# Cross stage: the parts of q and k in one DRAM array, stored by one transfer; the stacks loaded head by head

## The chip, the cores and the metric

The kernel runs on one core of one Trainium2 chip. The metric is the device time of one execution in microseconds (us).

## The reference

A decoder layer with normalisation after each block, on 32 sequences (batches) of 256 tokens and 256 features, and a context of 120 rows for each sequence:

```python
x = layernorm(x + self_attention(x))          # 16 heads of 16, rotary
x = layernorm(x + cross_attention(x, ctx))    # 16 heads, differential
x = layernorm(x + feed_forward(x))            # 64 experts, top 6, and a shared one
```

The change lies in the cross attention. There each head has two softmaxes:

```python
q1, q2 = (q[..., :8], q[..., 8:])             # q, k: heads of 16
k1, k2 = (k[..., :8], k[..., 8:])
a1 = softmax(einsum('bhtd,bhsd->bhts', q1, k1) * SCALING)
a2 = softmax(einsum('bhtd,bhsd->bhts', q2, k2) * SCALING)
out = einsum('bhts,bhsd->bhtd', a1 - lam * a2, v)
```

## The kernel before

The kernel has three stages, one after the other: self attention, cross attention, feed forward. The two attention stages are pipelines over the batches. In step t the cross stage loads x and ctx of batch t (X), projects q and k of batch t-1 (A), loads the stacks of batch t-2 and starts its maxima of the scores (B), finishes those of batch t-3 (M), computes scores, exponentials and values of batch t-4 (S), and later phases follow (O, R, Q). Each step of each engine is written out by hand, in eight sub-steps, and each engine works through its own list in order, waiting on semaphores.

To keep float32 accuracy in bf16 matmuls, q and k are split into three bf16 parts whose sum is the float32 value (`cparts`, made by `copy_parts0`, `copy_parts1` on ScalarE and two subtractions on GpSimd). A score is the sum of six products of parts. The six are laid below one another in a stack, so that one matmul with a contraction over 48 rows (6 pairs x 8 features) does them: `q_stack` and `k_stack`, 48 rows for each half `e` of the head (e = 0 at partition 0, e = 1 at partition 64), and along the free dimension all 16 heads, 256 queries or 120 keys each.

`cparts` has (feature, head) in the partitions, feature-major, and the stacks want the feature in the partition and the head in the free dimension. SyncE's queue makes this turn through DRAM: the phase A of a step stores the parts of batch t-1 (L586, L588), and the phase B of the next step loads them back as stack rows (L556), 7 loads for each e: of q 8, 8, 16 and 16 rows, of k 24, 16 and 8 rows (`C_STACK_LOADS`). Before the change each of q and k has its own DRAM array with e outermost, `[3, E, NP, P, T]` and `[3, E, NP, P, KEYS]` (3 slots, 2 halves, 3 parts, 128 rows of (feature, head), then queries or keys). There a stack row, one feature of all 16 heads, is a single run of 16 x 256 x 2 = 8192 bytes (q) or 16 x 120 x 2 = 3840 bytes (k).

SyncE issues in this order in a step: x and ctx for X, the residual for S, then, after the stores of the step before have landed (`c_pw`), the 14 stack loads for B; y and its transpose x2T for R; the three row loads of `cnmaxT` for M (L569, after ScalarE's copy); gates and counts for Q (L574, L576); and at last the four stores of parts for A, after `c_lo`. TensorE waits for all 14 loads (`c_st`) before `cross_max_scores(B, 0)` (L829), in the sixth of the eight sub-steps, and behind it come the other maxima, the transpose of the maxima L1021 that M needs, and the values. ScalarE's `copy_parts0` waits for the stores of the step before, since it overwrites `cparts`.

The self stage makes the same turn with arrays of its own, which the change does not touch.

Of the kernel before, what the change touches and what calls it, by code (L numbers as in the profile page):

```python
# [8 lines left out]
BF16 = mybir.dt.bfloat16  # L9
# [4 lines left out]
P = 128  # L14
DM = 256
T = 256
TC = T // P
FC = DM // P
NH = 16
# [3 lines left out]
NP = 3  # L23
# [11 lines left out]
def past(b, n):  # L35

    return True if not isinstance(b, int) else b >= n
# [7 lines left out]
def held(eng, count):  # L45


    if isinstance(count, int):
        return count
    register = eng.alloc_register()  # L50
    eng.reg_mov(register, count)
    return register
# [50 lines left out]
def attention(nc, n_batches, x_in, xT_in, W, ctxT_in, CW, consts, y_out, res_out, z_out, yT_out, counts_out, moe, ident, ahead, count):  # L103
# [24 lines left out]
    for is_q in (True, False):  # L128
        part_of = [pair[0 if is_q else 1] for pair in PAIRS]
        at = 0  # L130
# [17 lines left out]
    KEYS = ctxT_in.shape[1]  # L148
    E = 2
# [5 lines left out]
    HALF = P // E  # L155
    KPAD = P - KEYS
    QW, KW = E * T, E * KEYS
# [6 lines left out]
    for is_q in (True, False):  # L164
        part_of = [pair[0 if is_q else 1] for pair in PAIRS]
        at = 0
# [9 lines left out]
    cres_rows = res_out.rearrange("(b c p) d -> b p c d", p=P, c=TC)  # L176
    ctxT_rows = ctxT_in.rearrange("(b f p) n -> b p f n", f=FC, p=P)
    cy_rows = z_out.rearrange("(b c p) d -> b p c d", p=P, c=TC)
    cq_dram = nc.dram_tensor("cross_q_parts", [3, E, NP, P, T], BF16, kind="Internal").ap()
    ck_dram = nc.dram_tensor("cross_k_parts", [3, E, NP, P, KEYS], BF16, kind="Internal").ap()  # L180

    with ExitStack() as ctx:
        def sb(label, shape, dt=F32):
            return ctx.enter_context(nc.sbuf_tensor(f"att_{label}", shape, dt))
# [3 lines left out]
        def sem(label):  # L188
            sems.append(nc.alloc_semaphore(f"att_{label}"))
            return sems[-1]  # L190
# [28 lines left out]
        q_stack = sb("q_stack", [P, 3, NH * T], BF16)  # L219
        k_stack = sb("k_stack", [P, 3, NH * T], BF16)  # L220
# [41 lines left out]
        cparts = parts[:, :, :, :, :].rearrange("p z t c n -> p (z t c n)")[:, 0:NP * (QW + KW)]\  # L262
# [93 lines left out]
        c_pw = [sem(f"cross_parts_written{p}") for p in range(3)]  # L356
        c_st = [sem(f"cross_stacks_loaded{p}") for p in range(3)]
# [53 lines left out]
        def _(sp):  # L411
# [100 lines left out]
            def cross_step(at_lag):  # L512
                X, A, B, M, S, R, Q = (at_lag(lag) for lag in (0, 1, 2, 3, 4, 6, 7))
# [26 lines left out]
                        sp.wait_ge(c_sum, S.n - 2)  # L540
                    sp.dma_start(x_res[:, S.slot, :, :], cres_rows[S.n]).then_inc(c_res_in[S.slot], 16)
                if B.on:
                    n_pw = held(sp, 64 * (B.turn + 1))
                    sp.wait_ge(c_wts, 16)
                    sp.wait_ge(c_pw[B.slot], n_pw)

                    if not past(B.n, 3):
                        sp.wait_ge(c_ones, B.n + 1)
                    if past(B.n, 3):
                        sp.wait_ge(c_sc, NGR * (B.n - 2))  # L550
                    for e in range(E):
                        q_src = cq_dram[B.slot][e].rearrange("t (d h) n -> (t d) (h n)", h=NH)
                        k_src = ck_dram[B.slot][e].rearrange("t (d h) n -> (t d) (h n)", h=NH)
                        for is_q, row, src_row, m in C_STACK_LOADS:
                            stack, src, n = (q_stack, q_src, T) if is_q else (k_stack, k_src, KEYS)
                            sp.dma_start(stack[e * HALF + row:e * HALF + row + m, B.slot, 0:NH * n],  # L556
                                         src[src_row:src_row + m, :]).then_inc(c_st[B.slot], 16)
                if R.on:
                    sp.wait_ge(c_y, R.n + 1)
                    sp.dma_start(cy_rows[R.n][:, :, 0:DM], y_sb[:, R.slot, :, :]).then_inc(c_stored[R.slot], 16)  # L560
# [17 lines left out]
                if A.on:  # L578
                    n_lo = held(sp, A.n + 1)
                    sp.wait_ge(c_wts, 16)  # L580
                    sp.wait_ge(c_lo, n_lo)

                    if past(A.n, 3):
                        sp.wait_ge(c_st[A.slot], 16 * C_N_ST * A.turn)
                    for e in range(E):
                        sp.dma_start(cq_dram[A.slot][e].rearrange("t p n -> p t n"),  # L586
                                     cparts[:, :, e * T:(e + 1) * T]).then_inc(c_pw[A.slot], 16)
                        sp.dma_start(ck_dram[A.slot][e].rearrange("t p n -> p t n"),  # L588
                                     cparts[:, :, QW + e * KEYS:QW + (e + 1) * KEYS]).then_inc(c_pw[A.slot], 16)

            run_both(sp, step, cross_step, n_batches, LAGS, C_LAGS)
            sp.wait_ge(c_ahead, 16 * (len(ahead) + P // n_batches))
            sp.wait_ge(s_zero, 16 * len(moe) * (n_batches + 1))
# [471 lines left out]
        def _(act):  # L1065
# [125 lines left out]
            def copy_parts0(A, last):  # L1191
                act.wait_ge(c_ke, 2 * (A.n + 1))
                act.wait_ge(c_qe, 2 * (A.n + 1))

                if past(A.n, 1):
                    act.wait_ge(c_pw[last.slot], 64 * (last.turn + 1))
                else:
                    for p in range(3):
                        act.wait_ge(s_pw[p], 32 * len(range(p, n_batches, 3)))
                act.activation(cparts[:, 0, :], cqk[:, :], ACT.Copy).then_inc(c_hi, 1)  # L1200
# [5 lines left out]
            def cross_step(at_lag):  # L1206
# [59 lines left out]
                if A.on and not shared(A):  # L1266
                    copy_parts0(A, at_lag(2))
# [38 lines left out]
                if A.on and shared(A):  # L1306
                    copy_k(A)
                    copy_parts0(A, at_lag(2))
# [920 lines left out]
```

## Time and profile before

| | |
|---|---|
| time, median of 3 runs | 1919.88 us (1917.16 to 1926.09) |
| the profiled execution: time | 1924.67 us |
| the profiled execution: span | 1922.6 us |
| mean granted TensorE clock | 0.946 |
| TensorE busy | 1690.0 us (88%) |
| VectorE busy | 1310.4 us (68%) |
| share of the 16 DMA engines that SyncE's queue takes | 62.0% |

PE is TensorE's matmuls, PEld its weight loads, DVE VectorE, ACT ScalarE, POOL GpSimd, SP SyncE; a q behind a name is the engine's queue of issued transfers. L829 is line 829 of the kernel. The cross stage runs from about 720 to 1520 us of the span; from 830 to 1410 us all its phases are active. "Busy" leaves out issuing and waiting; a DMA packet is one piece that one of the 16 engines moves, and the share of the DMA is the mean over the 16.

### The profile page before, as it was taken

Reading aid. Unit: us, or ns where it says so; the run is one execution under the profiler, and the core shown is the slowest. Engines: PE = TensorE matmul, PEld = TensorE weight load, DVE = VectorE, ACT = ScalarE, POOL = GpSimd, SP = SyncE. Lnnn points to the kernel's source line nnn. Section 1 sums busy time; section 2 is a strip of 40 time slices with the busy share of each in tenths; the row PEclk is TensorE's granted clock in tenths of the full one; section 3 lists DMA queues with packets and bytes.
Section 4 is the critical chain, followed back from the end, with each engine's and each line's share of the span. In section 5 each row is a group of like instructions: output and inputs, shape, how many; then the busy total and the mean of one; then the engine's idle time right before and its main releaser. Section 6 shows DMA issues by size and latency. Waiting matters only on the chain. (4 is left out here: it accounts for less than half of the span.)

```text
span 1922.6 us, 43658 instructions
## 1 busy us (share of the span) xinstructions
PE 1690.0 (88%) x14562; PEld 1183.5 (62%) x14562; DVE 1310.4 (68%) x2959; ACT 1083.8 (56%) x1701; POOL 858.5 (45%) x788
## 2 busy tenths in 40 slices
PE   3789999999999997889989989999898749999985
PEld 2566667666666665555556555555555438888774
DVE  3566776777666775668888887988888544444275
ACT  1466666666666665567777777777776501111244
POOL 4567776777666742211212111111211005887565
PEclk6899999999999999899999999999998759999998
DMA  5577767776777666566655566566664326887686
GB/s 121 132 190 184 193 168 196 188 188 170 195 189 188 169 172 144 123 119 132 139 132 128 127 129 125 136 133 141 135 125 87 90 59 177 197 195 196 178 292 218
DMA packets 312751, 302.79 MB, mean 157 GB/s; under 512 B 68842, under 2 KB 289836, under 8 KB 303304
## 3 DMA queue, kind: packets, MB, share of 16 engines
q1 hardware_dynamic: 302408, 288.66, 62.0%
q0 software_dynamic: 10240, 12.81, 3.9%
q8 instruction: 59, 0.97, 0.2%
q14 instruction: 44, 0.36, 0.1%
HBM read 188.36 MB, written 112.00 MB: 156 GB/s over the span
## 5 line engine op out<-in xcount | busy, mean ns | idle before, releaser
L1340 DVE TENSOR_REDUCE att_nmax<-self_p_mx 128x2 f32<-128x512 f32 x512 | 328.8, 686 | 203.3 <-PE self_p_mx L629 202.8
L1430 DVE TENSOR_REDUCE att_cross_nmax<-self_p_mx 128x8 f32<-128x960 f32 x256 | 294.4, 1150 | 86.5 <-PE self_p_mx L829 85.4
L1074 ACT ACTIVATE att_probs<-self_p_sc 128x1024 f32<-128x1024 f32 x256 | 261.3, 1021 | 98.5 <-PE self_p_sc L617 96.2
L1167 ACT ACTIVATE att_probs<-self_p_sc 120x1024 f32<-120x1024 f32 x256 | 261.9, 1023 | 65.4 <-PE self_p_sc L811 64.5
L629 PE MATMUL self_p_mx<-att_k_stack,att_q_stack 96*128 96x256 bf16 x1024 | 160.8, 277 | 54.5 <-DMA att_k_stack<-self_k_parts 49.2
L847 PE MATMUL self_p_pv<-att_probs,att_v_aug 120*32 120x256 f32 x2048 | 172.3, 410 | 0.0
L617 PE MATMUL self_p_sc<-att_q_stack,att_k_stack 99*128 99x256 bf16 x1024 | 158.5, 278 | 11.4 <-ACT att_probs L1074 10.0
L829 PE MATMUL self_p_mx<-att_k_stack,att_q_stack 48*128 48x120 bf16 x2048 | 101.2, 220 | 70.6 <-DMA att_k_stack<-cross_k_parts 37.9
L1683 POOL TENSOR_SCALAR att_cross_var_eps<-att_cross_mv 128x2 f32<-128x2 f32 x32 | 7.2, 226 | 332.3 <-DVE att_cross_mv L1536 289.7
L1697 POOL TENSOR_TENSOR att_qk_rest<-att_qk,att_parts 128x752 f32<-128x752 f32 x32 | 51.8, 1619 | 214.3 <-ACT att_parts L1200 214.3
L629 PEld LDWEIGHTS self_p_mx<-att_k_stack,att_q_stack 96*128 96x128 bf16 x1024 | 96.0, 98 | 82.9 <-DMA att_k_stack<-self_k_parts 35.3
L617 PEld LDWEIGHTS self_p_sc<-att_q_stack,att_k_stack 99*128 99x128 bf16 x1024 | 87.1, 98 | 91.1 <-ACT att_probs L1074 42.7
L644 PE MATMUL self_p_pv<-att_probs,att_v_aug 128*32 128x256 f32 x2048 | 141.9, 396 | 0.5 <-ACT att_probs L1074 0.5
L829 PEld LDWEIGHTS self_p_mx<-att_k_stack,att_q_stack 48*128 48x128 bf16 x2048 | 70.0, 97 | 107.5 <-DVE att_cross_nmax L1430 56.2
L1904 PE MATMUL ffn_p<-shared_w,ffn_hT 128*128 128x256 f32 x512 | 122.3, 393 | 12.4 <-ACT ffn_hT L1967 12.0
L1913 PE MATMUL ffn_ph<-ffn_xT,shared_w 128*128 128x256 f32 x512 | 118.9, 386 | 0.0
L1904 PEld LDWEIGHTS ffn_p<-shared_w,ffn_hT 128*128 128x128 f32 x512 | 97.9, 196 | 31.3 <-ACT ffn_hT L1967 17.5
L1637 POOL TENSOR_TENSOR att_rope_products<-att_qkb,att_cos_t 128x512 f32<-128x512 f32 x32 | 40.9, 1279 | 154.8 <-ACT att_qkb L1090 154.8
L2090 POOL DMA_INDIRECT expert_sums<-ffn_ye,ffn_slots x64 | 92.3, 1442 | 37.3 <-issue 14.7
L1177 ACT ACTIVATE att_o_raw<-self_p_pv 128x512 f32<-128x512 f32 x128 | 75.8, 592 | 56.3 <-PE self_p_pv L847 56.3
L1701 POOL TENSOR_TENSOR att_parts<-att_qk_rest,att_parts 128x752 bf16<-128x752 f32 x32 | 51.7, 1614 | 124.9 <-ACT att_parts L1204 124.9
L1967 ACT ACTIVATE ffn_hT<-ffn_ph 128x512 f32<-128x512 f32 x64 | 37.7, 594 | 121.5 <-PE ffn_ph L1913 87.8
(180 smaller groups left out, 3682.4 us busy)
## 6 DMA issues: line engine op xcount, KB each, us to landing
att_q_stack<-self_q_parts SPq DMA_DIRECT2D x64, 256.0 KB, 5.7
expert_sums<-att_zeros SPq DMA_DIRECT2D x64, 256.0 KB, 8.7
att_q_stack<-cross_q_parts SPq DMA_DIRECT2D x128, 128.0 KB
ffn_w<-in_ffn_w SPq DMA_DIRECT2D x64, 256.0 KB
ffn_m_sb<-expert_sums SPq DMA_DIRECT2D x32, 512.0 KB, 6.0
self_q_parts<-att_parts SPq DMA_DIRECT2D x32, 384.0 KB
self_k_parts<-att_parts SPq DMA_DIRECT2D x32, 384.0 KB
att_k_stack<-self_k_parts SPq DMA_DIRECT2D x32, 384.0 KB, 7.9
```

Of the source, the lines that this page charges most:

```text
L617: mm = pe.matmul(p_sc[:, w, kc * T:(kc + 1) * T], k_stack[0:RM, S.slot, k_at:k_at + P], q_stack[0:RM, S.slot, u * T:(u + 1) * T], start=Tr ...
L629: mm = pe.matmul(p_mx[:, m % 2, c * T:(c + 1) * T], q_stack[0:RK, M.slot, q_at:q_at + P], k_stack[0:RK, M.slot, m * T:(m + 1) * T], start= ...
L644: mm = pe.matmul(p_pv[j * SLOT:(j + 1) * SLOT, (p % 2) * T:(p % 2 + 1) * T], v_aug[:, S.slot, kc, u, :], probs[:, (u // 2) % 4, (2 * (u % ...
L829: mm = pe.matmul(p_mx[:, e, (2 * hh + c) * KEYS:(2 * hh + c + 1) * KEYS], q_stack[r:r + C_RK, M.slot, q_at:q_at + P], k_stack[r:r + C_RK, ...
L847: mm = pe.matmul(p_pv[j * SLOT:(j + 1) * SLOT, (g % 2) * T:(g % 2 + 1) * T], v_aug[0:KEYS, S.slot, e, 2 * g + hh, :], probs[0:KEYS, g % 4, ...
L1074: act.activation(probs[:, g % 4, :], p_sc[:, :, :].rearrange("p b n -> p (b n)"), ACT.Exp, scale=SCALE).then_inc(s_exp, 1)
L1167: act.activation(probs[0:KEYS, g % 4, :], p_sc[0:KEYS, :, :].rearrange("p b n -> p (b n)"), ACT.Exp, scale=C_SCALE).then_inc(c_exp, 1)
L1340: dve.tensor_reduce(nmax[:, M.slot, :, m], p_mx[:, m % 2, :].rearrange("p (c k) -> p c k", c=TC), AX_X, ALU.max, negate=True).then_inc(s_r ...
L1430: dve.tensor_reduce(cnmax[:, M.slot, :, :, 2 * m:2 * m + 2].rearrange("p c e h -> p e h c"), p_mx[:, :, 0:4 * KEYS].rearrange("p e (x k) - ...
L1904: mm = pe.matmul(p_y[:, tc * DM:(tc + 1) * DM], hT[:, b % 2, k, tc * P:(tc + 1) * P], sw2[:, k, :], start=(k == 0), stop=(k == SK - 1))
L1913: mm = pe.matmul(p_h[:, k // 2, (k % 2) * T:(k % 2 + 1) * T], sw1[:, f, k * P:(k + 1) * P], xT[:, t % 3, f, :], start=(f == 0), stop=(f == ...
L2090: pool.indirect_dma_start(out=moe[j][:, :], out_offset=bass.IndirectOffsetOnAxis(ap=slots[:, e:e + 1], axis=0), in_=ye[:, k % 3, j, :], in ...
```

## The change

The two DRAM arrays become one, `cross_parts`, `[3, NP, P, QW + KW]`: for each part and each (feature, head) one run of 2 x 256 + 2 x 120 = 752 elements (1504 bytes), as `cparts` has it. One transfer stores it, in place of four, and the counts of `c_pw` go from 64 to 16 for each batch. The 14 stack loads stay, with the same rows; each reads 16 runs (one for each head) of 512 or 240 bytes for a stack row, 1504 bytes apart.

```diff
--- before.py
+++ after.py
@@ -176,8 +176,7 @@
     cres_rows = res_out.rearrange("(b c p) d -> b p c d", p=P, c=TC)
     ctxT_rows = ctxT_in.rearrange("(b f p) n -> b p f n", f=FC, p=P)
     cy_rows = z_out.rearrange("(b c p) d -> b p c d", p=P, c=TC)
-    cq_dram = nc.dram_tensor("cross_q_parts", [3, E, NP, P, T], BF16, kind="Internal").ap()
-    ck_dram = nc.dram_tensor("cross_k_parts", [3, E, NP, P, KEYS], BF16, kind="Internal").ap()
+    c_dram = nc.dram_tensor("cross_parts", [3, NP, P, QW + KW], BF16, kind="Internal").ap()
 
     with ExitStack() as ctx:
         def sb(label, shape, dt=F32):
@@ -540,7 +539,7 @@
                         sp.wait_ge(c_sum, S.n - 2)
                     sp.dma_start(x_res[:, S.slot, :, :], cres_rows[S.n]).then_inc(c_res_in[S.slot], 16)
                 if B.on:
-                    n_pw = held(sp, 64 * (B.turn + 1))
+                    n_pw = held(sp, 16 * (B.turn + 1))
                     sp.wait_ge(c_wts, 16)
                     sp.wait_ge(c_pw[B.slot], n_pw)
 
@@ -548,13 +547,13 @@
                         sp.wait_ge(c_ones, B.n + 1)
                     if past(B.n, 3):
                         sp.wait_ge(c_sc, NGR * (B.n - 2))
+                    by_row = c_dram[B.slot].rearrange("t (d h) n -> (t d) h n", h=NH)
                     for e in range(E):
-                        q_src = cq_dram[B.slot][e].rearrange("t (d h) n -> (t d) (h n)", h=NH)
-                        k_src = ck_dram[B.slot][e].rearrange("t (d h) n -> (t d) (h n)", h=NH)
                         for is_q, row, src_row, m in C_STACK_LOADS:
-                            stack, src, n = (q_stack, q_src, T) if is_q else (k_stack, k_src, KEYS)
-                            sp.dma_start(stack[e * HALF + row:e * HALF + row + m, B.slot, 0:NH * n],
-                                         src[src_row:src_row + m, :]).then_inc(c_st[B.slot], 16)
+                            stack, at, n = (q_stack, e * T, T) if is_q else (k_stack, QW + e * KEYS, KEYS)
+                            dst = stack[e * HALF + row:e * HALF + row + m, B.slot, 0:NH * n]
+                            sp.dma_start(dst.rearrange("p (h n) -> p h n", h=NH),
+                                         by_row[src_row:src_row + m, :, at:at + n]).then_inc(c_st[B.slot], 16)
                 if R.on:
                     sp.wait_ge(c_y, R.n + 1)
                     sp.dma_start(cy_rows[R.n][:, :, 0:DM], y_sb[:, R.slot, :, :]).then_inc(c_stored[R.slot], 16)
@@ -582,11 +581,8 @@
 
                     if past(A.n, 3):
                         sp.wait_ge(c_st[A.slot], 16 * C_N_ST * A.turn)
-                    for e in range(E):
-                        sp.dma_start(cq_dram[A.slot][e].rearrange("t p n -> p t n"),
-                                     cparts[:, :, e * T:(e + 1) * T]).then_inc(c_pw[A.slot], 16)
-                        sp.dma_start(ck_dram[A.slot][e].rearrange("t p n -> p t n"),
-                                     cparts[:, :, QW + e * KEYS:QW + (e + 1) * KEYS]).then_inc(c_pw[A.slot], 16)
+                    sp.dma_start(c_dram[A.slot].rearrange("t p n -> p t n"), cparts[:, :, :])\
+                      .then_inc(c_pw[A.slot], 16)
 
             run_both(sp, step, cross_step, n_batches, LAGS, C_LAGS)
             sp.wait_ge(c_ahead, 16 * (len(ahead) + P // n_batches))
@@ -1193,7 +1189,7 @@
                 act.wait_ge(c_qe, 2 * (A.n + 1))
 
                 if past(A.n, 1):
-                    act.wait_ge(c_pw[last.slot], 64 * (last.turn + 1))
+                    act.wait_ge(c_pw[last.slot], 16 * (last.turn + 1))
                 else:
                     for p in range(3):
                         act.wait_ge(s_pw[p], 32 * len(range(p, n_batches, 3)))
```

## Rows read from the trace of the kernel before

**Rows 1.** The page: the span, and busy time of each engine (share of span, instructions)

```profile
span 1922.6 us, 43658 instructions
PE 1690.0 (88%) x14562; PEld 1183.5 (62%) x14562; DVE 1310.4 (68%) x2959; ACT 1083.8 (56%) x1701; POOL 858.5 (45%) x788
```

**Rows 2.** The waits, whole span: us in total, times, longest us

```profile
PE self_p_mx L829 <- DMA att_k_stack<-cross_k_parts: 37.9, 23, 6.3
...
PEld self_p_mx L829 <- DMA att_k_stack<-cross_k_parts: 16.5, 8, 6.6
```

**Rows 3.** The waits, 830 to 1410 us

```profile
PE self_p_mx L829 <- DMA att_k_stack<-cross_k_parts: 27.2, 19, 2.9
...
PEld self_p_mx L829 <- DMA att_k_stack<-cross_k_parts: 4.1, 3, 1.9
```

**Rows 4.** The waits of SyncE's queue, 830 to 1410 us

```profile
SPq L569 <- ACT att_cross_nmaxT L1314: 168.9, 25, 9.5
...
SPq L545 <- DMA cross_k_parts<-att_parts: 14.2, 14, 1.7
SPq L550 <- DMA cross_k_parts<-att_parts: 6.3, 5, 1.9
```

**Rows 5.** The windows: busy time of the engines, 830 to 1410 us

```profile
core 0: us, PE busy (x) PEld busy (x) DVE busy (x) ACT busy (x) POOL busy (x), PEclk, DMA share, GB/s
830.00:1410.00 580.00, 527.32 (x5750) 337.58 (x5750) 492.61 (x1146) 421.96 (x702) 114.92 (x150) 0.98 0.63 132
```

**Rows 6.** The timeline of SyncE's queue: start us, us

```profile
1033.41 1.70 SPq L569 DMA_DIRECT2D att_q_stack<-att_cross_nmaxT  x3
...
1036.77 0.40 SPq L586 DMA_DIRECT2D cross_q_parts<-att_parts  x1
...
1038.31 0.51 SPq L588 DMA_DIRECT2D cross_k_parts<-att_parts  x1
1039.16 0.38 SPq L532 DMA_DIRECT2D att_xT<-x  x1
...
1042.05 1.46 SPq L556 DMA_DIRECT2D att_q_stack<-cross_q_parts  x4
...
1046.21 1.13 SPq L556 DMA_DIRECT2D att_k_stack<-cross_k_parts  x3
```

**Rows 7.** The timeline of TensorE: start us, us; in brackets the idle time before

```profile
1053.80 0.39 PE L829 MATMUL self_p_mx<-att_k_stack,att_q_stack 48*128 48x120 bf16 x8 [0.70 <-DMA att_k_stack<-cross_k_parts]
...
1055.18 0.28 PE L1021 MATMUL self_p_k<-att_identb,att_cross_nmax_parts 128*96 128x128 bf16 x2
```

**Rows 8.** The DMA view, 288.5 to 290.5 us (the self stage stores its parts)

```profile
DMA packets 1037, 0.52 MB, mean 261 GB/s; under 512 B 16, under 2 KB 1037, under 8 KB 1037
...
q1 hardware_dynamic: 1037, 0.52, 89.2%
```

**Rows 9.** The DMA view, 302.7 to 303.7 us (rows of 1024 bytes)

```profile
DMA packets 388, 0.37 MB, mean 375 GB/s; under 512 B 22, under 2 KB 388, under 8 KB 388
...
q1 hardware_dynamic: 388, 0.37, 108.1%
```

**Rows 10.** The DMA view, 1038.4 to 1038.9 us (a store of k parts)

```profile
DMA packets 419, 0.11 MB, mean 214 GB/s; under 512 B 378, under 2 KB 419, under 8 KB 419
...
q1 hardware_dynamic: 419, 0.11, 96.2%
```

**Rows 11.** The DMA view, 1037.4 to 1040.4 us (the four stores)

```profile
q1 hardware_dynamic: 1606, 0.58, 75.0%
```

**Rows 12.** The DMA view: issues, KB each, us from issue to landing (median)

```profile
cross_q_parts<-att_parts SPq DMA_DIRECT2D x64, 192.0 KB, 2.7
...
x<-att_y_sb SPq DMA_DIRECT2D x32, 256.0 KB, 4.2
...
cross_k_parts<-att_parts SPq DMA_DIRECT2D x64, 90.0 KB, 3.0
```

**Rows 13.** The DMA view, 1043.3 to 1052.8 us (the stack loads)

```profile
DMA packets 734, 1.57 MB, mean 165 GB/s; under 512 B 201, under 2 KB 479, under 8 KB 639
...
q1 hardware_dynamic: 734, 1.57, 87.4%
```

**Rows 14.** The DMA view, 830 to 1410 us

```profile
DMA packets 90961, 76.63 MB, mean 132 GB/s; under 512 B 40468, under 2 KB 82935, under 8 KB 88535
```

## The prediction

> **What bounds the kernel now.** I read the page first. TensorE is busy 88% of the span, no other engine over 68% [rows 1]. So a change in the transfers counts only where TensorE waits for them. The list of waits gives two rows that end on `cross_k_parts`, the stack loads of the cross stage: 23 waits of TensorE's matmuls (37.9 us) and 8 of its weight loads (16.5 us), 31 waits and 54.4 us in all, for 32 batches [rows 2]. That is nearly one wait for each batch, and 54.4 us is the most that any relief can give.
>
> Next I asked for the steady part, 830 to 1410 us. SyncE's queue waits 25 times for `cross_nmaxT` there [rows 4], once a step, so a step takes 580/25 = 23.2 us. TensorE is busy 527.32 of the 580 us [rows 5]. 22 of the 25 steps have the wait for the stacks, 31.3 us together, 1.4 us each [rows 3]. The timelines of one step show why it recurs [rows 6, 7]. After `max_scores(B, 0)` comes the transpose L1021, then ScalarE copies `cross_nmaxT`, then SyncE issues in order: the three row loads (1033.41), the gates and counts, four stores of parts (1036.77 to 1038.82), the loads of x and ctx and the residual, and, once the stores have landed, 14 stack loads (1042.05 to 1047.34). The last lands near 1053.8, where TensorE resumes after 0.70 us. So it is a loop: in the 22 steps that wait now, whatever makes the stacks land later makes the step longer by the same amount, and what makes them land earlier shortens it until the wait is gone.
>
> **The change, part by part.** Two things move: the stores get fewer and larger pieces, the loads get more and smaller ones. I need the time of a piece. While only 512-byte pieces move, 1037 packets fill 89.2% of 16 engines for 2.0 us [rows 8]: 0.892 x 16 x 2000 / 1037 = 27.5 ns for a mean of 501 bytes. In the 1024-byte stretch it is 1.081 x 16 x 1000 / 388 = 44.6 ns for 954 bytes [rows 9]. A line through both: 8.6 ns for each piece, and 0.0377 ns for each byte. It gives 18.5 ns for the 240-byte stores, where the row has 0.962 x 16 x 500 / 419 = 18.4 ns (mean 263 bytes) [rows 10]. So, alone, a piece costs: 240 bytes 17.6 ns, 512 bytes 27.9, 1504 bytes 65.3, 3840 bytes 153, 8192 bytes 317 (the last three by extending the line).
>
> *The store.* Before: 4 transfers, 128 x 3 x 2 pieces of 512 and as many of 240 bytes, 1536 pieces; in the stretch of the stores 0.750 x 16 x 3.0 = 36 engine-us, 2.25 us for all 16 [rows 11]. After: 384 pieces of 1504 bytes, 384 x 65.3 / 16 = 1.57 us. SyncE issues one instruction in place of four: it is free 1.54 us earlier (1036.77 to 1038.31) [rows 6]. The stack loads wait for the landing, though. Before, the last store is issued 1.54 us after the first and lands in 3.0 us: 4.5 us. The q store lands in 2.7 us [rows 12] with 384 x 27.9 / 16 = 0.67 us of moving, so about 2.0 us are fixed; the one store should land 2.0 + 1.57 = 3.6 us after its issue. Gain 0.9 us. Bounds: at least 0.5 us (its fixed part is larger by as much as the x store's 4.2 us suggests [rows 12], which moves 256 KB beside other work), at most 1.54 us plus SyncE's present wait for the parts, (14.2 + 6.3) / 25 = 0.8 us [rows 4], so 2.3 us. I take 0.9.
>
> *The loads.* Still 14, same bytes, same rows of the stacks. But a stack row no longer lies in one run in DRAM: it is 16 runs of 512 bytes (q) or 240 bytes (k), 1504 bytes apart. Before, a row is one packet: of 734 packets in the stretch of the loads, 734 - 639 = 95 are of 8 KB or more [rows 13], and there are 96 q rows. 192 pieces become 3072. Alone they would cost 96 x (317 + 153) = 45.1 engine-us before and 1536 x (27.9 + 17.6) = 69.9 after. They are not alone now: the stretch holds 0.874 x 16 x 9.5 = 132.8 engine-us, of which the other 542 packets and 0.415 MB take 542 x 8.6 ns + 0.415 MB x 0.0377 = 20.3. That leaves 112.5 engine-us for the stack rows, 2.5 times what they need alone: they hold each other up. No row tells whether small pieces are held up as much, so I bound it:
> - lowest, no holding up at all: 69.9 - 112.5 = -42.6 engine-us; at 16 x 0.874 = 14 engines, -3.0 us a step;
> - highest, the same factor 2.5: 69.9 x 2.5 = 174.4, +61.9, so +4.4 us;
> - between, the bytes held up as before and the fixed 8.6 ns added for each of 2880 new pieces: +24.8 engine-us, +1.8 us.
>
> I take +1.8 us, since the fixed part is the one thing that three rows agree on [rows 8 to 10]. SyncE's time for the 14 issues (5.3 us) may grow: a store of 384 pieces takes 0.51 us, a stack load some 0.37 [rows 6]. At 0.51 us each it would be 7.1 us, still inside the 9.5 us that the engines need, so it costs nothing; if that cover went, it would be up to 1.8 us. The y and x2T stores behind them would go later, but SyncE then waits 7 us for `cross_nmaxT` (168.9 / 25) [rows 4], which covers it. ScalarE's `copy_parts0` waits for the store of a step ago and is covered by most of a step. No wait is added.
>
> *Sum.* Each step: -0.9 + 1.8 = +0.9 us. It counts in the 31 waits: 31 x 0.9 = +28 us. The profiled execution has a span of 1922.6 us and a time of 1924.67, 4.8 us above the median of the runs. 1924.67 + 28 = 1952.7 on its own terms, and 1919.88 + 28 = 1948 us against the median.
>
> **The rivals.** What a measurement here can tell from no change is about 0.5%, 9.6 us, or 0.31 us a step.
>
> *Rival 1, faster: the fixed part hides.* The loads of 8 and 16 rows write few partitions, and a row takes 2.5 times its own time. If what holds them up is the place where they write, an engine that handles its fixed 8.6 ns lets another move bytes, and the stream keeps its length. Then the loads add 0 and the step gains 0.9 us: 31 x -0.9 = -28 us, 1892 us. It decides where the loads grow by under 0.6 us. For it: the factor 2.5 itself. Against it: the stretch is at 0.874, not 1 [rows 13], so not every engine is held up all the time, and where it isn't its own time counts. The Trainium skill ("SBUF — State Buffer", The DMA port swizzle) says that DMA bandwidth follows how many of 16 ports the partitions reach, four neighbours sharing one; by it 8 rows reach two ports, and the sum would be this rival's. The factor 2.5 agrees with it. The case with no holding up at all (-3.0 us) would end all waits, at most -54 us, 1866 us.
>
> *Rival 2, much slower: pieces are held up like rows, or small ones cost double.* With the factor 2.5 the step grows by 4.4 - 0.9 = 3.5 us: +109 us, 2029 us. A milder form: only the k pieces cost twice, 1536 x 17.6 ns = 27 engine-us or 1.9 us more, +28 + 60 = 2008 us. For it: their source and target offsets are multiples of 32 and 16 bytes only. Against it: the 240-byte stores lie on the line of the others [rows 10]. The Trainium skill ("DMA: Bandwidth & Descriptors", Specifications) gives 512 bytes as the least for full rate and says that below it the engine reads, modifies and writes; by it the milder form would come true. The trace disagrees for stores to DRAM (18.4 ns), and has no small-piece load into few partitions.
>
> *Rival 3, no change:* the loads grow by 0.6 to 1.2 us and the store pays for it; 1920 us.
>
> **How the numbers follow.** Forecast (slower by 10 to 60 us): 0.35. Rival 2: 0.18. Rival 3: 0.17. Rival 1: 0.30, of it 0.05 for a relief beyond 28 us. So faster 0.30, same 0.17, slower 0.53. The time is that of the likeliest, 1948 us; its own range is 1930 to 1980. The whole range must hold 8 in 10: from 1886, which leaves out the strong relief, to 2008, which leaves out the upper half of rival 2.
>
> **What would show it.** In the profile after: TensorE's wait for `cross_parts` at L829 grows from 54.4 to about 80 us, the time from the store's issue to the first stack load falls from 5.3 to about 4.3 us, and the stack loads' stretch grows from 9.5 to some 11.3 us while the packets of the steady part rise by 25 x (2880 - 1152), from 90961 [rows 14] to some 134,000. If the stretch stays at 9.5 us, rival 1 was right. If the store lands no earlier, the gain of 0.9 us is wrong. If the waits end on something else than the stacks, the loop is.

## The result

The changed kernel takes 2013.63 us (median of 4 runs, 2003.48 to 2015.58) against 1922.99 us beside it: ratio 1.0463, 95% interval 1.0416 to 1.0511. It is slower by some 90 us, where I had forecast 28 and a range up to 2008. Its profiled execution has a span of 2012.2 us and a mean granted clock of 0.922. Of the kernels below, one execution (the changed kernel with alternating loads, 2403.80 us at a clock of 0.645) was in a slow state and is left out of its time and ratio.

The page of the changed kernel: the span, busy time of each engine, the packets of the whole span, the landing of the one store.

```profile
span 2012.2 us, 43562 instructions
PE 1720.5 (86%) x14562; PEld 1206.7 (60%) x14562; DVE 1293.5 (64%) x2959; ACT 1088.1 (54%) x1701; POOL 857.8 (43%) x788
...
DMA packets 366511, 302.78 MB, mean 150 GB/s; under 512 B 91883, under 2 KB 349741, under 8 KB 360137
...
cross_parts<-att_parts SPq DMA_DIRECT2D x32, 564.0 KB, 3.4
```

The work of the engines is what it was, but TensorE's busy time grew by 30 us for the same 14562 matmuls, a first hint that some of them ran at a lower clock. The bytes are the same. The store lands in 3.4 us; I had worked out 3.6.

The waits of the changed kernel, whole span, and below them those of 830 to 1410 us (us in total, times, longest).

```profile
PE self_p_mx L825 <- DMA att_k_stack<-cross_parts: 111.0, 32, 9.5
...
PEld self_p_mx L825 <- DMA att_k_stack<-cross_parts: 44.8, 11, 9.8
```

```profile
PE self_p_mx L825 <- DMA att_k_stack<-cross_parts: 82.0, 23, 9.5
...
PEld self_p_mx L825 <- DMA att_k_stack<-cross_parts: 28.1, 6, 9.8
```

Here a reading of the prediction must be put right. The rows of PE and of PEld tell of the same moments: a weight load and its matmul wait for the same stacks, and both are listed. One such moment in the timeline of the changed kernel (in brackets the idle time before):

```profile
878.74 0.49 PE L825 MATMUL self_p_mx<-att_k_stack,att_q_stack 48*128 48x120 bf16 x8 [3.34 <-DMA att_k_stack<-cross_parts]
...
878.73 0.24 PEld L825 LDWEIGHTS self_p_mx<-att_k_stack,att_q_stack 48*128 48x128 bf16 x8 [3.62 <-DMA att_k_stack<-cross_parts]
```

All 11 waits of PEld after the change, and 7 of the 8 before, end within 0.02 us of one of PE's. So they must not be added: TensorE waited 37.9 us in 23 steps before (and 0.4 us in one more), not 54.4 us in 31, and waits 111.0 us in all 32 now. In the steady part it is 27.2 us in 19 of 25 steps against 82.0 us in 23 waits. The loss lies in the cross stage: from the first stack load of the first batch to that of the last it took 727.9 us and takes 819.7, 91.8 us more. The wait that the prediction had named grew by 73.1 us, and TensorE's busy time by the 30 us above; other waits gave a little back.

SyncE's queue in one step (start us, us), and the DMA view of that step's stack loads.

```profile
1043.88 0.40 SPq L584 DMA_DIRECT2D cross_parts<-att_parts  x1
...
1047.32 2.79 SPq L555 DMA_DIRECT2D att_q_stack<-cross_parts  x4
1050.16 2.15 SPq L555 DMA_DIRECT2D att_k_stack<-cross_parts  x3
1052.35 2.65 SPq L555 DMA_DIRECT2D att_q_stack<-cross_parts  x4
1055.04 2.13 SPq L555 DMA_DIRECT2D att_k_stack<-cross_parts  x3
1057.46 0.42 SPq L559 DMA_DIRECT2D x_and_gates<-att_y_sb  x1
...
1065.97 1.74 SPq L568 DMA_DIRECT2D att_q_stack<-att_cross_nmaxT  x3
```

```profile
DMA packets 3720, 1.68 MB, mean 123 GB/s; under 512 B 1738, under 2 KB 3651, under 8 KB 3720
...
q1 hardware_dynamic: 3720, 1.68, 93.1%
```

From the store to the first stack load it is 3.4 us now, where it was 5.3 [rows 6]. The 14 issues take 9.85 us, where they took 5.3. The window of the loads is 1048.6 to 1062.3 us, 13.7 us where it was 9.5 [rows 13], at a higher share of the engines: 0.931 x 16 x 13.7 = 204 engine-us (one engine-us is one of the 16 DMA engines busy for 1 us) against 132.8.

Three means over the steps of the steady part, read off the timelines of SyncE and TensorE, tell the step apart. I use them for every kernel below. *Store to load* is from the first store's start to the first stack load's; *load to maxima* from there to the matmuls that end their wait for the stacks (steps without that wait are left out); *step* is from one first stack load to the next.

| us | store to load | load to maxima | step |
|---|---|---|---|
| before | 5.1 | 12.5 | 23.1 |
| changed | 3.6 | 16.3 | 26.2 |

-1.5 and +3.9 make +2.4 us; the step grew by 3.0. The rest is behind the wait. Windows of the changed kernel around one wait (the columns as in [rows 5]):

```profile
1050.00:1060.00 10.00, 9.68 (x99) 6.85 (x100) 8.15 (x20) 8.31 (x16) 2.97 (x5) 1.00 1.01 113
1060.00:1062.80 2.80, 0.64 (x7) 0.19 (x5) 1.54 (x4) 2.78 (x6) 0.00 (x0) 1.00 0.77 152
1062.80:1067.00 4.20, 4.19 (x42) 2.35 (x42) 2.70 (x5) 1.70 (x3) 1.61 (x1) 0.59 0.03 10
1067.00:1072.00 5.00, 5.00 (x59) 3.20 (x55) 4.31 (x14) 1.98 (x4) 0.00 (x0) 1.00 0.47 138
```

After 2.2 us in which TensorE waited, the mean granted clock is 0.59 for 4.2 us, mostly the lower of its two levels (1.2 of 2.4 GHz), and TensorE is busy all of that time. These matmuls lie in the loop, ahead of the transpose that SyncE's row loads wait for:

```profile
1062.81 0.39 PE L825 MATMUL self_p_mx<-att_k_stack,att_q_stack 48*128 48x120 bf16 x8 [2.17 <-DMA att_k_stack<-cross_parts]
...
1065.03 0.42 PE L1017 MATMUL self_p_k<-att_identb,att_cross_nmax_parts 128*96 128x128 bf16 x2
```

From the maxima to the transpose it is 2.22 us, where it was 1.38 for the same matmuls [rows 7]. Over the waits of the steady part the mean is 2.18 us against 1.47: these 0.7 us are the rest. The clock over the 4.2 us behind the wait was 0.64 or less after 22 of the 23 waits of the changed kernel, and 0.69 or less after 5 of the 19 of the kernel before. Before, a wait of 0.70 us left the clock at 1.00:

```profile
1053.80:1058.00 4.20, 4.20 (x49) 2.92 (x50) 3.90 (x6) 3.55 (x7) 1.62 (x1) 1.00 0.03 10
```

### The profile page after: what moved, and what is told of

Read it like the earlier page. It is cut to its first block and busy times, and to the rows that moved or that the text cites. A ratio compares the mean times of both kernels' runs of the same rounds, so it can differ in the third digit from the quotient of the medians.

```text
span 2012.2 us, 43562 instructions
## 1 busy us (share of the span) xinstructions
PE 1720.5 (86%) x14562; PEld 1206.7 (60%) x14562; DVE 1293.5 (64%) x2959; ACT 1088.1 (54%) x1701; POOL 857.8 (43%) x788
## 5 line engine op out<-in xcount | busy, mean ns | idle before, releaser
L825 PE MATMUL self_p_mx<-att_k_stack,att_q_stack 48*128 48x120 bf16 x2048 | 107.6, 230 | 130.9 <-DMA att_k_stack<-cross_parts 111.0
L843 PE MATMUL self_p_pv<-att_probs,att_v_aug 120*32 120x256 f32 x2048 | 184.6, 436 | 0.0
L825 PEld LDWEIGHTS self_p_mx<-att_k_stack,att_q_stack 48*128 48x128 bf16 x2048 | 78.4, 103 | 160.2 <-issue 76.2
L1900 PE MATMUL ffn_p<-shared_w,ffn_hT 128*128 128x256 f32 x512 | 122.1, 393 | 13.1 <-ACT ffn_hT L1963 12.7
L807 PE MATMUL self_p_sc<-att_q_stack,att_k_stack 51*128 51x256 bf16 x1024 | 108.3, 293 | 2.7 <-ACT att_probs L1163 2.7
```

The costliest lines, as they stand in the source:

```text
L807: mm = pe.matmul(p_sc[:, e, hh * T:(hh + 1) * T], k_stack[r:r + C_RM, S.slot, h * KEYS:h * KEYS + P], q_stack[r:r + C_RM, S.slot, h * T:(h ...
L825: mm = pe.matmul(p_mx[:, e, (2 * hh + c) * KEYS:(2 * hh + c + 1) * KEYS], q_stack[r:r + C_RK, M.slot, q_at:q_at + P], k_stack[r:r + C_RK, ...
L843: mm = pe.matmul(p_pv[j * SLOT:(j + 1) * SLOT, (g % 2) * T:(g % 2 + 1) * T], v_aug[0:KEYS, S.slot, e, 2 * g + hh, :], probs[0:KEYS, g % 4, ...
L1900: mm = pe.matmul(p_y[:, tc * DM:(tc + 1) * DM], hT[:, b % 2, k, tc * P:(tc + 1) * P], sw2[:, k, :], start=(k == 0), stop=(k == SK - 1))
```

## The experiments

At first I had three theories of the longer loads. *Piece theory*: a piece keeps a DMA engine longer than its share of a row did. *Issue theory*: SyncE needs 0.70 us for a load in place of 0.38, and that delays the stacks. *Rule theory*: only pieces below 512 bytes cost more. Each ratio below is to runs of the kernel before on the same chip.

**Only q in pieces, only k in pieces.** The edit, in words of the loads: a kind in pieces has one array with both halves and one store, the other keeps its two arrays.

```diff
-    c_dram = nc.dram_tensor("cross_parts", [3, NP, P, QW + KW], BF16, kind="Internal").ap()
+    cq_dram = nc.dram_tensor("cross_q_parts", [3, NP, P, QW], BF16, kind="Internal").ap()
+    ck_dram = nc.dram_tensor("cross_k_parts", [3, E, NP, P, KEYS], BF16, kind="Internal").ap()
```

> Only q goes head by head (one q array, one store; the eight q loads read 512-byte runs). k keeps its arrays, its two stores and its loads of whole rows. Piece theory (small pieces keep the DMA engines longer, each kind by what the trace of the changed kernel shows: q from 73.6 to 96.7 engine-us a step, k from 39.9 to 84.4): the loads grow by 23/14 = 1.6 us a step, the stores give back some 0.5, so +35 us against the kernel before, 1958 us. Issue theory (SyncE's queue needs 9.8 us in place of 5.3 for the 14 loads, and that is what delays the stacks): 8 of the 14 loads are slower to issue, so over half of the loss, +50 us or more, 1973 us. Rule theory (only pieces below 512 bytes cost more): no loss, 1910 to 1923 us.

> Only k goes head by head (one k array, one store; the six k loads read 240-byte runs), q keeps its arrays, its two stores and its loads of whole rows. Piece theory: +44.5 engine-us, 3.1 us a step, less 0.5: +80 us against the kernel before, 2003 us. Issue theory: 6 of 14 loads are slower to issue, under half of the loss, +38 us, 1961 us. Rule theory: the whole loss, +90 us, 2013 us.

q in pieces: 2012.26 us, ratio 1.0497 (1.0443 to 1.0551). k in pieces: 1931.58 us, 1.0109 (1.0042 to 1.0175). q alone makes the whole loss. None of the three had a size for that: the piece theory had k as the dearer kind, the issue theory had q, but priced it at about half (1973 us), and the rule theory had no loss from q. The means say why.

| us | store to load | load to maxima | step |
|---|---|---|---|
| q in pieces | 4.9 | 15.0 | 26.0 |
| k in pieces | 3.9 | 13.7 | 23.3 |

The loads' part adds up: +2.5 for q and +1.2 for k, 3.7 of the 3.9. But k's pieces are paid for by its one store (480-byte runs in place of 240-byte ones: 1.2 us sooner), and q's one store gives nearly nothing (0.2 us), since the two k stores still come after it. Rule theory is out as the only cause, since the 512-byte pieces delay the maxima more than the 240-byte ones. The packet records tell the other half: in the steady part a 512-byte piece takes 62.7 ns in the changed kernel, where its sixteenth of an 8192-byte row took 47.8, and a 240-byte piece 55.2 in place of 26.1. In time of the DMA engines the small pieces grew most (44.6 of the 67.3 engine-us that a step's stack loads gained), and in the time to the maxima the large ones did.

**More issues, the same rows.**

```diff
+                            sp.dma_start(tiny[:, B.slot, k_tiny, :], consts["ident"][0:1, 0:16]).then_inc(c_tiny[B.slot], 16)
+                            k_tiny += 1
```

> The kernel before, with a transfer of 64 bytes into an unused tile issued after each of the 14 stack loads. The queue needs about 28 x 0.35 = 9.8 us for the loads, as in the changed kernel, while rows still travel whole. Issue theory: the stacks land some 3 to 4 us later in each step, +90 us or more, 2010 us. Piece theory: the engines have a backlog of rows anyway and the stacks land at most 1 us later, 0 to +25 us, 1920 to 1948 us.

1938.25 us, ratio 1.0119 (1.0090 to 1.0147). Load to maxima 13.1 us (+0.6), step 23.7 (+0.6), though the issuing took 8.9 us. The issue theory explains some 0.6 of the 3.9 us, no more; the piece theory stands, with the two kinds in the other order, though the cover that I had claimed for the issuing is not whole.

**Four stores again.**

```diff
-                    sp.dma_start(c_dram[A.slot].rearrange("t p n -> p t n"), cparts[:, :, :])\
-                      .then_inc(c_pw[A.slot], 16)
+                    rows = c_dram[A.slot].rearrange("t p n -> p t n")
+                    for e in range(E):
+                        for at, n in ((e * T, T), (QW + e * KEYS, KEYS)):
+                            sp.dma_start(rows[:, :, at:at + n], cparts[:, :, at:at + n]).then_inc(c_pw[A.slot], 16)
```

> The changed kernel, but its array is stored by four transfers again (q and k of each half). The trace of the changed kernel has 3.59 us from the store to the first stack load, that of before 5.09. If the stacks are what each step waits for, the 1.5 us come back in 31 or 32 steps: +47 us against the changed kernel, 2060 us. If the one store had brought nothing, 2014 us.

2050.72 us, ratio 1.0697 (1.0641 to 1.0753), where the changed kernel has 1.0463. The store's part of the change does bring 0.023 of the time, some 45 us by the ratios (37 us between the plain medians, which come from two chips), where 47 was expected. Only 1.0 of the 1.5 us came back between store and load (4.6 us against 3.6), and the step grew by 1.0 us, to 27.2, as the loop says. Here the clock of the steady part is 0.88, against 0.91.

**Alignment.** Rows of the array 1536 bytes apart:

```diff
-    c_dram = nc.dram_tensor("cross_parts", [3, NP, P, QW + KW], BF16, kind="Internal").ap()
+    c_dram = nc.dram_tensor("cross_parts", [3, NP, P, 768], BF16, kind="Internal").ap()[:, :, :, 0:QW + KW]
```

> The changed kernel with the rows of its array 1536 bytes apart in place of 1504 (32 bytes of each row unused), so that every q run starts at a multiple of 512 bytes and the k runs of the first half at a multiple of 256. Alignment theory (runs that start anywhere cost more to read): the mean of a 512-byte packet in the loads falls from 62.9 ns to some 50 and most of the loss of the q pieces goes, 1960 us or less. Piece theory (the number of pieces and where they are written): no change, 2005 to 2020 us.

2017.85 us, ratio 1.0504 (1.0456 to 1.0552): no help. Where the runs start in DRAM isn't it.

**Half of the bytes.**

```diff
+                            cut = n // 2 if past(B.n, 3) else n
-                                         by_row[src_row:src_row + m, :, at:at + n]).then_inc(c_st[B.slot], 16)
+                                         by_row[src_row:src_row + m, :, at:at + cut]).then_inc(c_st[B.slot], 16)
```

> The changed kernel, but from the fourth batch on each piece of the stack loads carries only the first half of its bytes (256 and 120), as many pieces as before; the rest of the stacks keeps old data, so the output is not the reference's. Bytes held up at the place of writing: the packets fall to about half, the stretch from 13.9 us to the 10 us that the issuing needs plus 1.5, the stacks land 16.3 - 3.0 = 13.3 us after the first issue or sooner, and the step is as before or shorter, 1900 to 1930 us. Cost by piece, whatever its bytes: the stretch stays over 13 us, 1990 us or more.

1916.63 us, ratio 0.9997 (0.9976 to 1.0019), with as many pieces and 10.0 us of issuing. The stack loads' packets fell further than to half: a 256-byte piece took 21.2 ns and a 120-byte one 14.4, 54.6 engine-us a step in place of 181, close to what the line of the prediction has for a piece alone (18.3 and 13.1). In the steady part one wait of 0.2 us was left and the step was 22.7 us. The total does not fall below that of the kernel before, since the first three batches still load all their bytes: of its 19.1 us of waiting for the stacks 18.9 lie before 830 us, where the kernel before waits 10.2. So neither the number of pieces nor the issuing makes the loss by itself; the bytes must be there too, held up somewhere.

**The order of the stack loads, in the kernel before and in the changed one.**

```diff
-                    for e in range(E):
-                        for is_q, row, src_row, m in C_STACK_LOADS:
+                    for is_q, row, src_row, m in C_STACK_LOADS:
+                        for e in range(E):
```

> The kernel before, with the order of its 14 stack loads changed: first half, second half, first half, and so on, in place of seven and seven. If rows hold each other up because neighbours in the queue write into the same few places, the alternation between partitions below 48 and partitions from 64 on lowers the mean of an 8192-byte packet from 764 ns to 600 or less and the stretch from 9.9 to some 8 us: the wait of 1.4 us a step shrinks to about none, 1885 to 1895 us. If it is not the place, no change, 1910 to 1925 us.

> The changed kernel with the stack loads of the two halves alternating. If neighbours in the queue hold each other up at the place of writing, the pieces gain as the rows did or more (0.85 us a step and the clock's share): 1980 to 1990 us. If the pieces are limited by SyncE's issuing, 9.8 us either way, no change, 2005 to 2020 us.

Before with the halves alternating: 1907.74 us, ratio 0.9944 (0.9916 to 0.9973), TensorE's wait for the stacks in the steady part 5.4 us in place of 27.2. That lies between the two forecasts (1885 to 1895, or no change): an 8192-byte packet still takes 769 ns, as before (765) and not the 600 expected, and the gain is in the k rows (334 ns in place of 417). The step fell only from 23.1 to 22.8 us, so the wait was not the whole of what could be won. The changed kernel with them alternating: 1938.72 us, ratio 1.0118 (1.0064 to 1.0173): 0.034 of the time, some 66 us, is won back by the order alone, far more than I had expected, with the issuing as slow as ever (10.1 us). Load to maxima is 14.4 us in place of 16.3, and the steady clock 0.97 in place of 0.91. Here too it is the k pieces that gain (40.3 ns in place of 55.2), while the q pieces stay (61.8 against 62.7). How long the k pieces are held up depends on which transfers stand next to each other.

**Single transfers on a quiet chip**, ahead of the kernel before, 8 to 24 rows, whole or in 16 pieces:

```diff
+                for rows, step, size, cut, pitch in ALONE:
+                    sp.dma_start(dst, src).then_inc(c_alone, 16)
+                    sp.wait_ge(c_alone, 16 * n_alone)
```

> The kernel before with 32 transfers ahead of it, one at a time, into a tile that is not yet in use: 8, 16 or 24 rows of 8192 or 3840 bytes, whole or as 16 pieces, into neighbouring partitions or into partitions 4, 8 or 16 apart. The time of the rest is not of interest. If the place of writing is what holds the rows up: whole rows into 8 neighbours take over 550 ns each, whole rows 4 or 16 partitions apart some 310 ns; and pieces of 512 bytes into neighbours 40 ns or more, spread 28. If it is the source: no difference between neighbours and spread partitions, and the source rows 9216 bytes apart are quicker than those 8192 apart. If neither shows alone, only the traffic of several transfers at a time makes it.

The DMA view of four of them, 8 rows of 8192 bytes each (8 of the packets are the 4-byte counts): whole rows into neighbours (42 to 44 us), whole rows 16 partitions apart (49.2 to 51.3), pieces into neighbours (52 to 54.4), pieces 16 apart (57.4 to 59.3).

```profile
q1 hardware_dynamic: 16, 0.07, 8.5%
```

```profile
q1 hardware_dynamic: 16, 0.07, 7.6%
```

```profile
q1 hardware_dynamic: 136, 0.07, 9.3%
```

```profile
q1 hardware_dynamic: 136, 0.07, 11.5%
```

8 rows take 0.085 x 16 x 2.0 = 2.7 engine-us whole and 0.093 x 16 x 2.4 = 3.6 in pieces, 2.6 and 3.5 when spread: 0.34 us a row and 27 ns a piece, as the line of the prediction has it (317 and 27.9 ns). For pieces the place is no matter in any of the transfers (26.7 to 27.3 ns). For whole rows it is not quite settled: the other three transfers of 8 rows into neighbours took 437 to 453 ns a row, the four spread ones 311 to 366, but of 16 rows neighbours took 414 and 429 and spread ones 447 and 453. None comes near the 550 that the place theory asked for, so for single transfers both theories of this run fall, and its third line holds: it takes several at a time. It also showed that the issuing itself is dearer: some 0.3 us for whole rows into neighbours (the very first 0.40), 0.6 to 0.85 us for pieces into neighbours, with an empty queue.

**The 14 loads of a step as a burst on the quiet chip:**

```diff
+                for pieces, own_source, spread, alternate in BURSTS:
+                        first, step = SPREAD[(e, j)] if spread else (64 * e + row, 1)
+                        sp.dma_start(dst, src).then_inc(c_alone, 16)
+                    sp.wait_ge(c_alone, 16 * n_burst)
```

> The kernel before with bursts ahead of it: the 14 stack loads of a step with their sizes, rows and order, all issued at once into an unused tile while nothing else runs, whole rows and pieces, each in four forms: as in the two kernels; each transfer with a source of its own in DRAM (they no longer read the same rows); the rows spread over all partitions; the two halves alternating; and for pieces own source and spread together. The trace of the transfers one at a time had 27 ns for a 512-byte and 17.7 ns for a 240-byte piece, 330 to 450 ns for an 8192-byte row. Source theory (the three copies of a part are read from the same DRAM rows by transfers in flight together): own sources bring the pieces to under 35 and 22 ns and rows to under 450, spreading brings nothing. Place theory: spreading brings them there, own sources nothing. If the burst as in the kernels already shows 27 and 18 ns, it is neither, but the other traffic of the step.

The DMA view of three windows, each with one whole burst of 1.16 MB: rows as in the kernel before (1.6 to 13.9 us), pieces as in the changed one (50.6 to 66.6), pieces spread over all partitions (83.1 to 93.2).

```profile
q1 hardware_dynamic: 360, 1.16, 70.2%
```

```profile
q1 hardware_dynamic: 3240, 1.16, 76.0%
```

```profile
q1 hardware_dynamic: 3240, 1.16, 52.6%
```

| burst | first issue to all landed, us | 512-byte (8192) packet, ns | 240-byte (3840) packet, ns |
|---|---|---|---|
| rows, as before | 13.3 | (887) | (489) |
| rows, own sources | 13.0 | (839) | (481) |
| rows, spread | 10.6 | (403) | (219) |
| rows, halves alternating | 12.1 | (896) | (392) |
| pieces, as changed | 17.0 | 66.8 | 57.1 |
| pieces, own sources | 15.6 | 56.4 | 50.7 |
| pieces, spread | 11.0 | 33.6 | 20.8 |
| pieces, halves alternating | 14.1 | 59.3 | 42.1 |
| pieces, own sources and spread | 10.9 | 33.1 | 19.3 |

(First of two rounds; the second agrees within 0.8 us, except for the last row, behind which no burst follows there. The first column is from one burst's first issue to the next one's, the others are the mean lengths of the packet records.) The pieces take 0.760 x 16 x 16.0 = 195 engine-us, spread 0.526 x 16 x 10.1 = 85. Nothing else runs, so the step's other traffic isn't needed: the burst alone shows the whole effect, 3.7 us from rows to pieces. Spreading takes the holding-up of the pieces away almost wholly, at nearly the same issuing (9.2 us against 9.95); what is left is 11.0 us. For the rows it is less clean, since spread rows are also issued more slowly (9.0 us against 5.4). Own sources help the pieces by 1.4 us and the rows by 0.3. With both, the pieces gain nothing beyond the spreading. So the place theory holds for several transfers in flight, with a small part for the shared source of the pieces: the stacks lie in partitions 0 to 47 and 64 to 111, and up to 14 transfers write there at once.

**A way to a faster kernel.** The gates' and counts' issues moved behind the stores:

```diff
-                if Q.on:
-                    sp.wait_ge(c_prob, Q.n + 1)
```

> The kernel before, with SyncE's two issues for gates and counts moved behind the four stores of parts. In the trace of before the third part is ready at 1057.3 us and the first store is issued at 1059.3. If the step is the loop stores, stack loads, maxima, row loads, stores, the stores go out 1.3 to 1.5 us earlier and the wait of 1.4 us a step nearly goes: 25 to 35 us faster, 1885 to 1895 us. If the loop isn't what sets the step, no change.

1911.75 us, ratio 0.9970 (0.9946 to 0.9994), where 1885 to 1895 was expected. The stores go out sooner (4.2 us behind the maxima in place of 5.5), but the two issues now stand in front of the stack loads: store to load grew from 5.1 to 5.6 us. I had priced the move at one place of the queue alone. Put into the queue's idle time after the x2T store, with the alternating order:

> The kernel before with the stack loads of the two halves alternating, and with SyncE's two issues for gates and counts moved into the queue's idle time behind the store of x2T. Loop theory: the stores go out 1.3 us earlier with nothing put in front of the stack loads in exchange, and the loads are 0.85 us shorter; together more than the wait of 1.25 us a step, so the wait is gone in nearly all steps and the step is TensorE's and VectorE's own, 22.6 us or less: 1890 to 1903 us. If not the loop, as inter_before, 1908 us.

1906.95 us, ratio 0.9962 (0.9941 to 0.9983). That misses its range of 1890 to 1903 too. In the steady part no wait for the stacks is left, and the step is 22.6 us in place of 23.1. No kernel here came below that, also not the one with half of the bytes (22.7): once the stacks come in time something else sets the step, and no run here isolates what. So the steady step had 0.5 us to give, 31 x 0.5 = 16 us, and the expectations of 1885 to 1895 us had taken the whole wait, 1.4 us in each step that has one, for gain. The order alone (0.9944) had already taken what there was, and the intervals overlap. Both kernels with the alternating order are faster than the kernel before by about half a percent, and their intervals leave out 1.

## Why the prediction was wrong

- *What bounds the kernel, and the loop.* Right in kind; the counts were not. 31 waits and 54.4 us add the weight loads' waits to those of the matmuls behind them: it was 24 waits and 38 us, 19 of the 25 steady steps and not 22, and 1.1 us a step in the mean. So the most that a relief could give was 38 us by the waits, and 16 us by the steps. For the loss it mattered little, since all 32 steps wait now. Four stores in place of one, the order, and the change itself all moved the time through the wait at L829 (L825 after).
- *The one store, -0.9 us.* Right in kind, too small: 5.1 to 3.6 us is -1.5, inside its bounds of 0.5 to 2.3. The landing was close (3.4 against 3.6 us). It has a wait of its own left, 14.4 us in 22 steps.
- *The loads, +1.8 us: the step that failed.* They measured +3.9. The term that was mis-sized is "the fixed 8.6 ns added for each of 2880 new pieces", +24.8 engine-us a step. It measured +67: the packets of the stack loads took 114 engine-us a step before and 181 after, 14.9 ns more for a 512-byte piece than for its share of a row, and 29.1 ns more for a 240-byte one. My upper bound, "the same factor 2.5", gave 174.4 engine-us and +4.4 us. I chose the middle, bytes held up as before and the fixed 8.6 ns added once, since that was "the one thing that three rows agree on". But rows 8 and 10 are stores, whose bytes go to DRAM and not into a few partitions, and in none of the three do rows hold each other up as the stack loads do; for these only the bounds stood. The bursts show it: where many transfers write into few partitions, a 512-byte piece takes 66.8 ns in place of 887 / 16 = 55.4, and a 240-byte one 57.1 in place of 489 / 16 = 30.6.
- *The issuing "costs nothing".* Wrong in size and in cover. It takes 9.8 us and not 7.1 (the price of a store's instruction, 0.51 us, was the wrong row), and with rows alone a queue of 8.9 us costs 0.6 us a step (the run with more issues).
- *What the sum left out:* the clock. It falls behind nearly every wait (to 0.59 over 4.2 us in the stretch shown); -1.5 + 3.9 is 2.4 us, the step grew by 3.0, and the maxima-to-store part behind the wait grew from 5.5 to 6.3 us, all of it between the maxima and the transpose (1.47 to 2.18 us). Over 31 steps that is some 20 us of the 90. The sum for all, 31 x 3.0 = 93 us, meets the 89.6 between the two spans.
- *Rival 1 (the fixed part hides)* was half right, in the half that did not count. It had the place as the cause, and the bursts show that. Its conclusion, that pieces then cost nothing more, is wrong. The Trainium skill ("SBUF — State Buffer", The DMA port swizzle) ties bandwidth to the ports that the partitions reach; by its table the seven loads of one half reach 8 of the 16 ports and the two halves together all 16. The burst agrees in that alternating the halves brings the pieces from 17.0 to 14.1 us and spreading each transfer to 11.0. But the burst of 17.0 us reaches all 16 ports as well, so the ports of the whole do not give the time, and a transfer alone does not show them: pieces into 8 neighbours (27.0 ns) were as quick as spread ones.
- *Rival 2* named the size (the factor 2.5 kept, 2029 us), with the measured 2014 near it. In part that is luck: the loads came out lower than its +4.4 us, the store gave more than 0.9, and the clock, which it left out, added 0.7. The milder form (2008 us) came nearer still, and the k pieces did cost about twice their share of a row in the kernel (55.2 against 26.1 ns). But its reason, by the Trainium skill ("DMA: Bandwidth & Descriptors", Specifications: below 512 bytes read, modify, write), is not borne out: alone the 240-byte pieces take 18 ns, in the run with half of the bytes pieces of 256 and 120 bytes take 21 and 14 ns in the same partitions, and q in pieces of 512 bytes makes the whole loss without any small piece of k.

What stays open: what sets the step at 22.6 us, why a piece costs more than its bytes at a crowded place (66.8 against 55.4 ns, and 57.1 against 30.6), why the q pieces delay the maxima more although the k pieces gain more packet time, and why the alternating order helps pieces so much more than rows (2.9 against 1.2 us in the burst).

## What to carry to other kernels

Where transfers hold each other up, the time of a piece alone says nothing: scale what the crowded rows show, and keep a factor whose cause is unknown in the forecast instead of half of it. Before cutting a transfer's runs, ask where they are written: many transfers in flight into the same few partitions pay for every cut, and their order in the queue is worth a try first (0.6% on the tuned kernel for an exchange of two loops, 3.4% on the changed one). A longer wait of TensorE can cost more than itself: here the clock behind it came back lower, and the work in the loop took 0.7 us a step more. And before adding up the waits of a profile, see whether two rows tell of the same moment.

## What the runs showed of the hardware that I had not expected

- A transfer whose two sides have different shapes (a row on one, 16 runs on the other) takes SyncE 0.61 to 0.85 us to issue, with an empty queue, against some 0.3 us for whole rows into neighbouring partitions (0.27 to 0.33, the first 0.40). These are for neighbouring partitions; of the pieces into partitions further apart, the least was 0.53 us. Whole rows into partitions 4, 8 or 16 apart took 0.56 to 0.81 us as well.
- A single transfer in pieces runs as fast into 8 neighbouring partitions as into spread ones (27 ns a 512-byte piece), and whole rows at 0.33 to 0.45 us against 0.31 to 0.37; with 14 in flight a row took 887 ns in neighbours and 403 spread, a 512-byte piece 66.8 and 33.6.
- With as many pieces but half of the bytes the holding-up was gone: 21.2 ns for 256 bytes, where 512 bytes took 62.7.
- After a wait of 2.2 us the mean granted clock was 0.59 for 4.2 us of work without a gap, after 0.70 us it stayed at 1.00. The length of the wait did not decide it alone: in the kernel before it was 0.64 after a wait of 1.56 us and 1.00 after one of 1.94.
